# Moving contexts 2 and 6, and two transposed maxima, from odd steps to the even steps before them

## What is computed

```python
x = x + 0.5 * ffn(layernorm(x))          # 128 -> 512 -> 512 -> 128, weights +1/-1, relu
x = x + attention(layernorm(x))          # 16 heads of 8, softmax, then (ctx + x) layernormed, gamma, beta
x = x + 0.5 * ffn(layernorm(x))
# attention, per sequence and head:
attn = softmax(Q @ K.T / sqrt(8)); ctx = attn @ V
```

## Time and profile before

| what | value |
|---|---|
| median of 3 runs | 801.49 us (798.28 to 805.25) |
| profiled execution, its own time | 802.05 us |
| span of its instructions | 800.2 us |
| PE busy | 703.7 us, 88% of the span |
| DVE busy | 644.4 us, 81% |
| ACT busy | 511.0 us, 64% |
| POOL busy | 367.5 us, 46% |
| mean granted TensorE clock | 0.959 of full speed |

### The profile page before, as it was taken

The page is one execution under the profiler, slowest core; times in us unless marked ns, Lnnn a source line. Parts: engine busy times, 40 slices in busy tenths (PEclk is TensorE's granted clock), DMA queues, the critical chain, the costliest instruction groups (busy, mean ns, idle before and its releaser), DMA issues.

```text
span 800.2 us, 18450 instructions
## 1 busy us (share of the span) xinstructions
PE 703.7 (88%) x7258; PEld 333.9 (42%) x7258; DVE 644.4 (81%) x1244; ACT 511.0 (64%) x736; POOL 367.5 (46%) x654
## 2 busy tenths in 40 slices
PE   6779497999999999999999999999999999696887
PEld 2333233344444444444444444444444444242334
DVE  5548678798988888898988888898988888677755
ACT  3314466676767667776777666776767767566642
POOL 4522324528264653627273644627272742726320
PEclk8888698999999999999999999999999999799999
DMA  3011001010101101010101011010101001010000
GB/s 69 14 46 48 15 2 61 2 61 16 62 15 41 36 6 57 16 61 15 61 16 52 25 29 48 2 62 15 61 16 61 15 29 34 3 59 4 15 2 26
DMA packets 29508, 25.62 MB, mean 32 GB/s; under 512 B 4336, under 2 KB 29424, under 8 KB 29424
## 3 DMA queue, kind: packets, MB, share of 16 engines
q1 hardware_dynamic: 28992, 24.07, 9.5%
q10 hardware_dynamic: 432, 0.39, 0.1%
HBM read 5.05 MB, written 4.19 MB: 12 GB/s over the span
## 4 chain that ended last, share of the span: by engine, by line
PE 59%; DVE 22%; ACT 8%; issue 5%; POOL 5%; DMA 0%; POOLq 0%; SPq 0%; DVEq 0%; ACTq 0%
PE ps_z L635 13%; PE ps_z L636 12%; DVE ffn_lo L1204 9%; PE ps_c L798 8%; PE ps_s L747 6%; DVE row_max L1306 6%; PE ps_m L721 4%; ACT probs L1008 4%; PE ps_z L646 2%; ACT ffn_hi L970 2%; PE ps_z L619 2%; PE ps_z L648 2%; PE ps_m L732 2%; PE ps_m L810 2%; DVE att_bn L1181 2%
## 5 line engine op out<-in xcount | busy, mean ns | idle before, releaser
L1306 DVE TENSOR_REDUCE row_max<-ps_s 128x4 f32<-128x1024 f32 x256 | 312.4, 1220 | 64.3 <-PE ps_s L747 61.8
L1008 ACT ACTIVATE probs<-ps_t,score_scale 128x1024 f32<-128x1024 f32 x252 | 279.5, 1109 | 59.6 <-PE ps_t L760 56.6
L970 ACT ACTIVATE ffn_hi<-ps_z 128x512 f16<-128x512 f32 x270 | 156.6, 590 | 117.5 <-PE ps_z L636 82.4
L635 PE MATMUL ps_z<-ffn_hi,w 128*128 128x512 f16 x480 | 184.9, 385 | 6.5 <-DVE ffn_lo L1204 6.4
L1204 DVE SCALAR_TENSOR_TENSOR ffn_lo<-ps_z,ffn_hi 128x512 f16<-128x512 f32 x240 | 161.8, 684 | 28.6 <-ACT ffn_hi L970 28.5
L636 PE MATMUL ps_z<-ffn_lo,w 128*128 128x512 f16 x480 | 183.5, 382 | 0.0
L798 PE MATMUL ps_c<-probs,v_cols 128*32 128x256 f32 x2048 | 134.4, 391 | 0.9 <-ACT probs L1008 0.7
L747 PE MATMUL ps_s<-k_rows,q_rows 32*128 32x256 f16 x1024 | 103.1, 280 | 36.0 <-DVE row_max L1306 32.4
L760 PE MATMUL ps_t<-q_rows,k_rows 32*128 32x256 f16 x992 | 99.3, 279 | 0.0
L522 POOL TENSOR_TENSOR max_scaled<-row_max,max_unit 128x16 f32<-128x16 f32 x64 | 14.2, 222 | 156.3 <-DVE row_max L1306 156.3
L798 PEld LDWEIGHTS ps_c<-probs,v_cols 128*32 128x32 f32 x2048 | 57.5, 111 | 56.1 <-issue 29.3
(11 more groups left out here) (176 smaller groups left out, 1031.9 us busy)
## 6 DMA issues: line engine op xcount, KB each, us to landing
x<-L_attn_x SPq DMA_DIRECT2D x16, 256.0 KB, 2.7
q_rows<-q_hi SPq DMA_DIRECT2D x32, 128.0 KB, 2.5
y<-x SPq DMA_DIRECT2D x16, 256.0 KB, 2.1
k_rows<-k_hi SPq DMA_DIRECT2D x30, 128.0 KB, 2.1
q_rows<-q_lo SPq DMA_DIRECT2D x16, 128.0 KB, 2.1
q_rows<-no_max SPq DMA_DIRECT2D x16, 128.0 KB, 2.1
k_rows<-k_lo SPq DMA_DIRECT2D x15, 128.0 KB, 2.1
q_rows<-max_rows SPq DMA_DIRECT2D x64, 8.0 KB
```

Of the source, the lines that this page charges most:

```text
L635: pe.matmul(o[:], w, ffn_hi[:, 1 + k, :], start=(k == 0), stop=False)
L970: a_.activation(ffn_hi[:, use, :], ps_z[use % 2][:], ACT.Relu if use else ACT.Copy, scale=1.0 if use else XN_SCALE).then_inc(z_hi, 1)
L1008: a_.activation(probs[n % PROBS][:, j:j + 2, :], o[:], ACT.Exp, scale=score_scale[:, 0:1]).then_inc(s_exp, 1)
L1306: v.tensor_reduce(row_max[hb % 2][:].rearrange("p (a l) e -> p l a e", a=2)[:, j:j + 2, :, g % 2], ps_s[:].rearrange("p l (a k) -> p l a k ...
```

## The change

Two tables of numbers are changed. Context 2 moves from step 3 to step 2 and context 6 from step 19 to step 18; the transpose of the fourth maxima of the tile before moves from step 3 to step 2, and that of the second maxima of the tile itself from step 19 to step 18. The copies on ACT, which stand one step behind their transposes, move from steps 4 and 20 to steps 3 and 19. The last iteration has tables of its own (`AT_CONTEXT_EARLY`, `AT_MAX_EARLY`), which stay.

```diff
-AT_CONTEXT = {0: (0, 1), 3: (2,), 4: (3,), 16: (4, 5), 19: (6,), 20: (7,)}
+AT_CONTEXT = {0: (0, 1), 2: (2,), 4: (3,), 16: (4, 5), 18: (6,), 20: (7,)}
 AT_CONTEXT_EARLY = {0: (0, 1), 3: (2,), 5: (3,), 7: (4,), 8: (5,), 13: (6,), 16: (7,)}
 AT_CONTEXT_OWN = (21, 25, 29)
-AT_MAX = (10, 19, 26, 3)
+AT_MAX = (10, 18, 26, 2)
```

## The result

The changed kernel takes **820.63 us** (median of 4 runs, 819.57 to 821.24), the kernel before 801.91 us (4 runs, 798.28 to 805.25). The ratio is 1.0233, 95% interval 1.0187 to 1.0279: slower by 15 to 22 us. The forecast was 821.3.

A forecast was written before the change was run, and what follows sets the result against it. The DVE chain from the first ffn_lo to the maxima was taken to bound loop step 6. 12 x 0.83 + 12 x 0.82 = 19.8 us on 802.05 gave 821.9, less 0.56 for the median: 821.3 us, range 813 to 827.

The forecast's parts named there:

- Step 1: On PE, context 2 waits 0.25 us for ACT's copy of contexts 0 and 1, the input pair queued behind it.
- Steps 2 and 3: The first input pair starts at 412.43 instead of 411.09; 0.55 us of slack is used up, first ffn_lo 0.83 us late.
- the slack under the exponential: On ACT, ffn_hi waits for the exponential anyway, so the input pair could be 0.55 us late unnoticed.
- Step 4: On ACT, the maxima's copy now stands between both ffn_hi; it costs nothing, with 0.55 us of cover left.
- Step 5: PE saves one 0.10 us change of shape; scores of loop step 4 come 0.15 us late, counted neither way.
- Step 6, the sum: Scores of loop step 6 come 0.83 us late, the second half 0.82: 12 of each make 19.8 us.
- nothing was given back there: Rival: PE's waits at loop step 9 and ahead of the last output pieces swallow the delay; 4.6 us remain, 806.1; 5%.
- The clock stayed at 1.00: Rival: PE's added pauses lower TensorE's clock, 11.5 us more, 832.8 us; 4%.
- The copy did hold the context up: Rival, claiming the opposite: ACT's copy is in time and context 2 doesn't wait, 815.4 us; 8%.
- PE's weight-load share of 42%: A skill page's measure of PE's headroom: a later matmul could be made up for, a sum near 0; not adopted.

The follow-up runs named there:

- Run 3: The changed kernel with the four statistics between the two ffn_lo moved from steps 3 and 19 to 2 and 18: 804.06 us, 1.0032 of the kernel before.
- Run 2: The kernel before with only the transposed maxima moved to steps 2 and 18 and their ACT copies ahead of the second ffn_hi: 800.69 us, ratio 0.9992.
- run 1: The kernel before with only contexts 2 and 6 moved to steps 2 and 18, maxima left at 3 and 19: 819.23 us, ratio 1.0224.
- run 4: The kernel before with the statistics of steps 3 and 19 moved to steps 2 and 18: 800.65 us, ratio 0.9992.
- run 5: The kernel before with contexts 2, 3, 6, 7 moved later, to steps 4, 5, 20, 21: 801.37 us, ratio 1.0006.
- run 6: The kernel before with contexts 2, 3, 6, 7 at steps 4, 5, 20, 21 and statistics at 2 and 18: 797.99 us, ratio 0.9960.
- run 9: The kernel before with contexts at steps 4, 5, 20, 21, statistics at 2 and 18, first transposed maxima at 11 instead of 10: 793.62 us, ratio 0.9908.

## Why the prediction was right

- **Step 1, the context waits for the copy**: yes, and for a little more. 0.25 us was forecast with a release of 0.06 us, the context starts 0.11 us behind the copy's end and 0.29 behind where it could (417.36, 0.21 us behind the last scores, as for the input pair before). In total 5.7 us in 26 places, of which 25 are new (24 or 25 were forecast). The prediction says that such a wait isn't in the trace of before; one is, in iteration 14, where no input pair covers it, and there too the context starts 0.11 us behind the copy's end (677.99 + 0.38 to 678.48, rows below). With 0.11 for 0.06 the forecast delay would have been 0.88 us. The way from the context to the input pair is 0.03 us shorter than forecast (1.06 against 1.09), so two small errors cancel in part. Run 3 shows that the wait is not the loss itself; that its 0.29 us enter the delay of the pair is read from the rows, and no run takes the wait alone away.

```profile
677.99 0.38 ACT L1020 ACTIVATE ctx_t<-ps_c 128x256 f32<-128x256 f32 x1 [0.74 <-PE ps_c L798]
...
678.48 1.07 PE L798 MATMUL ps_c<-probs,v_cols 128*32 128x256 f32 x16 [0.22 <-issue]
```

- **Steps 2 and 3, the slack under the exponential**: the heart of it. `ffn_lo` comes 2.84 us behind the scores of step 2 instead of 1.99, late by 0.85; forecast 0.83. That a delay under the slack costs nothing and one beyond it costs the excess is shown by two points: the maxima alone (0.2 us) cost nothing, the contexts alone (1.29 us) cost 0.79. The slack is 0.50 us by that and by the changed kernel (1.35 us cost 0.85); the 0.55 of the prediction leaves out the 0.04 us from the pair's end to `ffn_hi`, which its sum does count.
- **Step 4, the copy on ACT**: no cost, as forecast. Run 2 shows it with the contexts in place; in the changed kernel the second `ffn_hi` ends at 420.68, 0.69 us before DVE's second `ffn_lo` starts (421.37).
- **Step 5**: the wait ahead of the second pair of late input matmuls is 0.49 us (forecast 0.5) and is not part of the sum, since the maxima end later still. PE's new waits ahead of contexts and input pairs, 5.5 and 11.9 us, add up to nearly the loss, but they are where PE stands while the chain is late: in run 1 the second is 4.4 us, and the loss nearly the same.
- **Step 6, the sum**: 0.84 and 0.81 us a half against 0.83 and 0.82; 12 of each make 19.8 us, the forecast's own figure. The runs show 18.7, and their interval of 15 to 22 holds both. In the two profiled runs 23 of the 24 halves are 0.81 to 0.85 us longer; the first half of iteration 2 is not (25.29 us, 25.33 before), in a stretch whose granted clock was 0.94, and 0.91 before. Their spans differ by 17.6 us only. The changed kernel's run was 2.0 us ahead when the FFN of iteration 0 began (61.02 against 63.04 us), up to where both have the same order; the mean granted clock of the first 64 us was 0.89, and 0.82 before. That the median comes within 0.7 us of the forecast is in part luck.
- **The rivals**: the waits at step 9 and ahead of the output pieces are to the tenth what they were (10.4 us for `ctx_n`, 5.6 us for `ffn_lo`), so nothing was given back there. The clock stayed at 1.00 with the added pauses, in every stretch from 160 to 670 us. The Trainium skill, page TensorE: Matmul & The Clock Gate, section "A second HAM failure mode: psum-queue depth-cycling", reports a swinging clock from short pauses between groups of matmuls; this trace does not show it, with new pauses of 0.2 and 0.5 us in each half. The copy did hold the context up.
- The reading that PE's weight-load share of 42% leaves room was rightly set aside: that share is 41% in the slower kernel, and the half iterations lost what the chain lost.

What the prediction didn't see is how near the next bound was. It named the DVE chain as what sets step 6; run 4 shows that ACT's chain to the third `ffn_hi` was level with it. Lengthening the first chain cost in full; shortening it alone gained nothing. The late contexts (run 5) and the early statistics (run 4), each worth nothing alone, gain 2.5 us together (run 6), and with the first maxima a step later 7.0 us (run 9). That later step was not run by itself.

## What to carry to other kernels

When work is moved ahead of a producer, look for the slack that the producer's result has on the next engine (here 0.5 us behind an exponential): a move within the slack was free here (run 2), a move beyond it was paid by the whole chain behind, once for every repetition (run 1). A stall that keeps its size can still have moved: compare the distance between two fixed points of the loop, not the idle time of the group that stalls. And before a chain is shortened, find the chain that is second, since the gain ends there.

## What was not expected of the hardware

PE started a context 0.11 us behind the end of the ACT copy that it waited for, and scores 0.06 us behind the end of DVE's maxima (421.96 + 1.22 to 423.24); the profile calls the first wait "issue", with no releaser. Nothing else.
